# A group norm and a displaced 3x3 filter in one core: the orders of five engines by kind of unit

## The reference

```
g = v.reshape(B_, G, C_ // G, H_, W_)
m = jnp.mean(g, axis=(2, 3, 4), keepdims=True)
s = jnp.var(g, axis=(2, 3, 4), keepdims=True)
v = ((g - m) / jnp.sqrt(s + 1e-5)).reshape(v.shape)
...
shifted = x[:, ch[:, None, None], iyc[:, :, None], ixc[:, None, :]] * mask
kern = jnp.exp(-(kx * kx + ky * ky) / (2.0 * SIGMA * SIGMA))
kern = kern / kern.sum(axis=(1, 2), keepdims=True)
out = lax.conv_general_dilated(shifted, kern_c[:, None], (1, 1), 'SAME', feature_group_count=C)
...
x = x + out
```

## Time and profile before

| | us |
|---|---|
| median of 3 runs | 1114.45 |
| the profiled execution, its own time | 1114.61 |
| its span, first to last instruction | 1112.8 |
| TensorE products, busy | 833.4 |
| VectorE, busy | 835.0 |
| ScalarE, busy | 661.0 |
| GpSimd, busy | 170.7 |
| mean granted TensorE clock | 0.872 of full |

### The profile page before, as it was taken

One profiled execution on the slowest core, in us unless ns is written; L12 is line 12 of the kernel. 1 busy time (PEld: TensorE's weight loads), 2 busy tenths in 40 slices (PEclk: granted clock), 3 DMA queues, 4 the chain that ended last, 5 costly groups with the idle time before them and its releaser, 6 DMA issues. The chain is left out here.

```text
span 1112.8 us, 9630 instructions
## 1 busy us (share of the span) xinstructions
PE 833.4 (75%) x2176; PEld 399.4 (36%) x2176; DVE 835.0 (75%) x565; ACT 661.0 (59%) x547; POOL 170.7 (15%) x204
## 2 busy tenths in 40 slices
PE   6976986678688698759848887888888686888710
PEld 2432433234343244324324443343444343443310
DVE  8187696976948768696784968787887858659685
ACT  0564546565477574766556666556566474666771
POOL 3103131012110303201211110111112101102010
PEclk9988898989799898888969899898999889788955
DMA  9737979898899797989799999999999897997936
GB/s 373 309 148 274 430 291 400 345 382 373 343 403 412 287 429 320 410 328 398 319 347 429 396 402 428 398 429 398 430 398 433 336 426 305 399 431 306 373 160 292
DMA packets 27818, 403.07 MB, mean 362 GB/s; under 512 B 3216, under 2 KB 3216, under 8 KB 3216
## 3 DMA queue, kind: packets, MB, share of 16 engines
q1 hardware_dynamic: 27792, 402.71, 88.6%
HBM read 201.38 MB, written 201.33 MB: 362 GB/s over the span
## 5 line engine op out<-in xcount | busy, mean ns | idle before, releaser
L243 PE MATMUL sum_ps<-xs,bands 128*128 128x512 f32 x1024 | 505.4, 651 | 23.9 <-DMA xs<-x_dram 23.9
L346 ACT ACTIVATE unused<-xs,small 128x4096 bf16 (+1 forms) x96 | 356.1, 3709 | 20.7 <-ACT small L339 7.7
L499 DVE SCALAR_TENSOR_TENSOR smooth<-frame,xs 128x1700 f32 (+5 forms) x96 | 163.6, 1704 | 220.7 <-ACT frame L320 141.6
L243 PEld LDWEIGHTS sum_ps<-xs,bands 128*128 128x128 f32 x1024 | 209.1, 210 | 270.9 <-issue 267.5
L243 PE MATMUL sum_ps<-xs,halves 128*128 128x512 f32 x512 | 246.3, 637 | 74.2 <-DMA xs<-x_dram 74.2
L313 ACT ACTIVATE frame<-xs,small (+1 forms) x96 | 223.4, 2327 | 130.7 <-DVE smooth L502 128.2
L209 POOL TENSOR_TENSOR small<-small 128x3 f32<-128x3 f32 x32 | 60.9, 1902 | 900.3 <-ACT small L352 900.3
L506 DVE SCALAR_TENSOR_TENSOR xs<-smooth,small,xs 128x1700 f32 (+5 forms) x96 | 163.6, 1704 | 36.5 <-POOL small L221 34.0
L243 PEld LDWEIGHTS sum_ps<-xs,halves 128*128 128x128 f32 x512 | 102.3, 204 | 216.8 <-issue 122.8
L502 DVE SCALAR_TENSOR_TENSOR smooth<-frame,xs,smooth 128x1700 f32<-128x1700 f32 (+5 forms) x96 | 163.5, 1704 | 3.4
L509 DVE SCALAR_TENSOR_TENSOR xs<-smooth,small,xs 128x594 f32 (+9 forms) x96 | 159.8, 1665 | 3.4
(11 more groups left out here) (81 smaller groups left out, 279.0 us busy)
## 6 DMA issues: line engine op xcount, KB each, us to landing
xs<-x_dram SPq DMA_DIRECT2D x96, 2048.0 KB, 14.7
out_dram<-xs SPq DMA_DIRECT2D x96, 2048.0 KB, 11.8
smooth<-offset_dram SPq DMA_DIRECT2D x1, 48.0 KB, 4.0
```

The costliest lines, as they stand in the source:

```text
L243: last = nc.tensor.matmul(sum_ps[:, :], (FIRST, SAME, SECOND)[i], slot_px(n, c * BANK, (c + 1) * BANK), start=(i == 0 and c == 0), stop=(i ...
L346: nc.scalar.activation(unused[:, :], xs[:, bass.ds(n % SLOTS * PIX, PIX)], ACT.Square, bias=neg_mean[:, i:i + 1], accum_out=squares[:, i:i ...
L499: V.scalar_tensor_tensor(sm, frame_window(-1), side_w[:, bass.ds(n, 1), 0], frame_window(0), ALU.mult, ALU.add).wait_op(frame_ready, done_ ...
```

## The change

Five edits in one:

1. VectorE loads the word of the next tile (`windows` has one more entry for it) between L499 and L502 of the present one, not ahead of the tile; the addresses of the weights come from one register.
2. ScalarE has two orders. `large_unit` (even units) takes `variances` first, then the fills of tiles 0 and 1 one behind the other, and only then `sum_means` of the next unit. `small_unit` (odd ones) keeps the old order except that the second square goes ahead of the fill of tile 2. The loop runs over pairs. `variances` also waits until the weights of the unit before are all written.
3. SyncE starts the loads in another order: none after the first and third tile of six, two after the second and the sixth, one after the fourth and fifth.
4. TensorE sums one tile of the light unit ahead of the heavy unit's variances and two behind them; around a light unit's variances it stays at two and one.
5. GpSimd makes the weights tile by tile: one operation for the unit and three for each tile, ten in all, and releases each tile by itself.

```diff
@@ SyncE @@
+            AGAIN = [(), (0, 1), (), (2,), (3,), (4, 5)]
             for n in range(TILES):
                 store(n)
-                if 1 <= n <= TILES - SLOTS:
-                    load(n - 1 + SLOTS)
+                for i in AGAIN[n % len(AGAIN)]:
+                    m = n - n % len(AGAIN) + i + SLOTS
+                    if m < TILES:
+                        load(m)
@@ GpSimd @@
                 V.tensor_tensor(rstd0, var, power, ALU.pow).then_inc(rstd_step, 1)
                 pool.wait_ge(rstd_step, STEPS * u + 1)
-                V.tensor_tensor(fix, rstd0, rstd0, ALU.mult).then_inc(rstd_step, 1)
-                ...
-                V.tensor_tensor(col_w[:, now * UT:(now + 1) * UT, :], base_w[:, u * UT:(u + 1) * UT, :],
-                                rstd.unsqueeze(2).to_broadcast([P, UT, 3]), ALU.mult).then_inc(col_w_ready, UT)
+                for i in range(UT):
+                    column = slice(i, i + 1)
+                    V.tensor_scalar(fix[:, column], var[:, column], rstd0[:, column], rstd0[:, column],
+                                    ALU.mult, ALU.mult).then_inc(rstd_step, 1)
+                    pool.wait_ge(rstd_step, STEPS * u + 2 * i + 2)
+                    V.tensor_scalar(rstd[:, column], fix[:, column], -0.5, 1.5,
+                                    ALU.mult, ALU.add).then_inc(rstd_step, 1)
+                    pool.wait_ge(rstd_step, STEPS * u + 2 * i + 3)
+                    if u >= 2 and i == 0:
+                        pool.wait_ge(tile_done, UT * (u - 1) + 1)
+                    V.tensor_scalar(col_w[:, now * UT + i, :], base_w[:, u * UT + i, :], rstd0[:, column],
+                                    rstd[:, column], ALU.mult, ALU.mult).then_inc(col_w_ready, 1)
@@ TensorE @@
             for u in range(UNITS):
+                ahead = 1 if u % 2 == 0 else 2
                 if u + 1 < UNITS:
-                    sums(u + 1, range(UT - 1))
+                    sums(u + 1, range(ahead))
                 variances(u)
                 if u + 1 < UNITS:
-                    sums(u + 1, range(UT - 1, UT))
+                    sums(u + 1, range(ahead, UT))
                     means(u + 1)
@@ ScalarE @@
-            def variances(u):
+            def variances(u, first=False):
                 act.wait_ge(var_ps_ready, u + 1)
+                if not first:
+                    act.wait_ge(col_w_ready, UT * u)
+            def large_unit(u, first=False):
+                variances(u, first)
+                fill_frame(u, 0)
+                next_fill(u, 0)
+                fill_frame(u, 1)
+                next_fill(u, 1)
+                sum_means(u + 1)
+                means(u + 1)
+                square(u + 1, 0)
+                fill_frame(u, 2)
+                next_fill(u, 2)
+                means_to_fill(u + 1)
+                square(u + 1, 1)
+                square(u + 1, 2)
+            def small_unit(u, ahead=True):
                 ...
                 if ahead:
                     means(u + 1)
                     square(u + 1, 0)
+                    square(u + 1, 1)
                 fill_frame(u, 2)
                 if ahead:
                     next_fill(u, 2)
                     means_to_fill(u + 1)
-                    square(u + 1, 1)
                     square(u + 1, 2)
+            with act.Fori(0, UNITS // 2 - 1) as pair:
+                small_unit(act.snap(2 * pair + 1))
+                large_unit(act.snap(2 * pair + 2))
+            small_unit(UNITS - 1, ahead=False)
@@ VectorE @@
                                        ).wait_op(frame_ready, done_count, "sem-ge").then_inc(half_smooth, 1)
+                dve.reg_load(entry, windows[0:1, bass.ds(done, 1)])
                 V.scalar_tensor_tensor(sm, frame_window(1), side_w[:, bass.ds(n, 1), 1], sm,
...
             def tile_of(n):
-                dve.reg_load(entry, windows[0:1, bass.ds(n, 1)])
                 dve.reg_mov(done_count, n + 1)
                 done = dve.snap(done_count, min_val=1, max_val=TILES)
-                weights = dve.snap(n % (2 * UT), min_val=0, max_val=2 * UT - 1)
+                dve.reg_mov(column, n % (2 * UT) * 3)
+                weights = dve.snap(column, min_val=0, max_val=(2 * UT - 1) * 3)
```

More of the change, by code:

```diff
@@ L91, in build @@
         rstd0, fix, rstd = (small[:, 18 + i * UT:18 + (i + 1) * UT] for i in range(3))
-        col_w = small[:, 27:45].rearrange("p (u k) -> p u k", k=3)
+        col_flat = small[:, 27:45]
+        col_w = col_flat.rearrange("p (u k) -> p u k", k=3)
         side_w = xs[:, SLOTS * PIX:SLOTS * PIX + 2 * TILES].rearrange("p (n k) -> p n k", k=2)
         base_w = sb("base_w", [P, TILES, 3])
-        windows = sb("windows", [P, TILES], i32)
+        windows = sb("windows", [P, TILES + 1], i32)
         fills = sb("fills", [P, TILES], i32)
@@ L203, in _ @@
             pool.wait_ge(table_ready, 1)
-            STEPS = 5
+            STEPS = 1 + 2 * UT
             def weights(u):
@@ L380, in _ @@
                 square(0, i, first=(i == 0))
-            unit_of(0)
+            large_unit(0, first=True)
             act.addr_align(256, max_nops=0)
-            with act.Fori(1, UNITS - 1) as u:
-                unit_of(u)
-            unit_of(UNITS - 1, ahead=False)
+            with act.Fori(0, UNITS // 2 - 1) as pair:
+                small_unit(act.snap(2 * pair + 1))
+                large_unit(act.snap(2 * pair + 2))
+            small_unit(UNITS - 1, ahead=False)
         @block.vector
@@ L458, in _ @@
                                     ALU.logical_shift_left))
-            chained(V.tensor_tensor(windows[:, :], parts[:, KIND], parts[:, TO], ALU.bitwise_or))
-            chained(V.tensor_tensor(windows[:, :], windows[:, :], parts[:, FROM], ALU.bitwise_or))
+            chained(V.tensor_tensor(windows[:, 0:TILES], parts[:, KIND], parts[:, TO], ALU.bitwise_or))
+            V.tensor_copy(windows[:, TILES:], parts[:, FROM, 0:1])
+            chained(V.tensor_tensor(windows[:, 0:TILES], windows[:, 0:TILES], parts[:, FROM], ALU.bitwise_or))
             dve.wait_ge(exps_ready, 1)
@@ L483, in _ @@
             done_count = dve.alloc_register("done_count")
+            column = dve.alloc_register("column")
             def smooth_tile(rows, cols, src, dst, n, done, weights):
@@ L505, in smooth_tile @@
                 dve.wait_ge(col_w_ready, done)
-                V.scalar_tensor_tensor(x_window(0, rows), sm, col_w[:, bass.ds(weights, 1), 1], x_window(0, rows),
+                V.scalar_tensor_tensor(x_window(0, rows), sm, col_flat[:, bass.ds(weights + 1, 1)], x_window(0, rows),
                                        ALU.mult, ALU.add
                                        ).wait_op(smooth_ready, done_count, "sem-ge").then_inc(centre_added, 1)
-                V.scalar_tensor_tensor(x_window(1, rows), sm[:, 0:rows - 1], col_w[:, bass.ds(weights, 1), 0],
+                V.scalar_tensor_tensor(x_window(1, rows), sm[:, 0:rows - 1], col_flat[:, bass.ds(weights, 1)],
                                        x_window(1, rows), ALU.mult, ALU.add
                                        ).wait_op(centre_added, done_count, "sem-ge").then_inc(above_added, 1)
-                V.scalar_tensor_tensor(x_window(0, rows - 1), sm[:, 1:rows], col_w[:, bass.ds(weights, 1), 2],
+                V.scalar_tensor_tensor(x_window(0, rows - 1), sm[:, 1:rows], col_flat[:, bass.ds(weights + 2, 1)],
                                        x_window(0, rows - 1), ALU.mult, ALU.add
@@ L540, in _ @@
             dve.reg_mov(slot, 0)
+            dve.reg_load(entry, windows[0:1, 0:1])
             dve.addr_align(256, max_nops=0)
```

1 line of the change is left out of this document (removed).

## The result

The changed kernel takes 1123.19 us, the median of four runs (1121.30 to 1123.59), against 1113.89 for the kernel before on the same chip (four runs, 1113.13 to 1116.01): a ratio of 1.0077, 95% interval 1.0058 to 1.0096, so 0.8% slower. The forecast was 1120.5 us, on a base of 1114.6: a change of +6.0 us, where the medians show +9.3 and the two profiled executions +6.7. The profiled execution took 1121.3 us, the lowest of the four, its span is 1119.1 against 1112.8, and the mean granted clock fell from 0.872 to 0.846.

What follows compares the result with a forecast made beforehand. Bound: a cycle of VectorE's release, ScalarE's squares, TensorE's variance products and last sums, and ScalarE's fills, without loads. Terms 2.2 + 1.9 + 3.9 - 2.0 = +6.0 us on 1114.6 gave 1120.5 us, range 1103 to 1133.

Steps and rivals of the forecast that it cites:

- Where the time is set: Cycle: VectorE's release in the heavy unit, ScalarE's squares, TensorE's variance products and last sums, ScalarE's fills and squares; no load.
- the six periods that the forecast named: Periods of units 4, 6, 12, 14, 24, 26, where ScalarE's sum (L330) comes after VectorE's release.
- Variances ahead of the heavy frame: ScalarE waits 1.8 us more before every heavy frame, VectorE's 1.52 us wait at L506 goes: +2.2 us for 12 heavy units.
- Heavy order: ScalarE fills tile 1 straight behind tile 0; light sum at +12.8, tile 2 later in some heavy units: +1.9 us.
- much slower: Rival: ScalarE's loop of two units and GpSimd's ten operations leave 0.5 us more issue a fill: 1132 us, chance 0.10.
- Pairs outside the four lighter ones, with the last light unit: The forecast's terms outside the four lighter pairs: variances +2.2, heavy order +1.9, last light unit -2.0 us.
- Last light unit: Two VectorE issue gaps shrink by 0.7 us each and a 0.7 us wait for weights goes: -2.0 us.
- The four lighter pairs: From 604 to 847 us: saving unusable, 7.2 us on top, less 3.0 of waits and 0.3 of the sum's place: +3.9 us.
- Loads two at a time: SyncE's loads go some 14 us earlier, but TensorE takes such tiles 8 us or more after landing: 0.
- Weights and word: GpSimd's tile-by-tile weights cost nothing under the heavy frame; VectorE's early word saves 0.7 us a gap, mostly off the cycle.
- The clock's rival: TensorE's shorter waits keep its clock high, sums at 7.1 us: -24 us, about 1097, or half, 1109; chance 0.20.
- Nothing moves: Rival: transfers hold the lighter pairs at 418 GB/s, gains and losses cancel against slack: 1114 to 1116 us, chance 0.18.

Runs made afterwards that it cites:

- e6: The changed kernel with SyncE's order of loads as before: 1115.53 us, ratio 1.0019 to the kernel before.
- e3: The changed kernel with TensorE summing two tiles ahead of every unit's variances, as before the change: 1110.94 us, ratio 0.9986 to the kernel before.
- e11: The changed kernel with SyncE's and TensorE's orders both as before: 1129.87 us, ratio 1.0135 to the kernel before.
- e12: e11 with the heavy unit's variances behind the fill of tile 0: 1094.05 us, ratio 0.9808 to the kernel before.
- e1: The changed kernel with the heavy unit's variances behind the fill of tile 0 again: 1117.32 us, ratio 1.0033 to the kernel before.
- e2: The changed kernel with all three tiles of the next heavy unit summed ahead of the light unit's variance products: 1093.07 us, ratio 0.9818 to the kernel before.
- e4: The kernel before with only the one edit of e2, three tiles summed ahead around light units: 1115.68 us, ratio 1.0022 to the kernel before.
- e5: The changed kernel with TensorE two tiles ahead at heavy units and three at light ones: 1094.55 us, ratio 0.9831 to the kernel before.
- e8: The changed kernel with the table word loaded ahead of its own tile again: 1125.18 us, ratio 1.0094 to the kernel before.
- e7: The changed kernel with GpSimd's six weight operations of before: 1122.85 us, ratio 1.0084 to the kernel before.

## Why the prediction was right, point by point

The four kernels that differ only in two of the edits say it best (medians in us, all with the variances first; the kernel before stood between 1112.9 and 1115.3 beside them):

| | loads as changed | loads as before |
|---|---|---|
| one ahead | 1123.2, ratio 1.0077 (the change) | 1115.5, 1.0019 (e6) |
| two ahead | 1110.9, 0.9986 (e3) | 1129.9, 1.0135 (e11) |

Each new order cures the variances' place by itself (e3, e6); both together do it twice and pay for both. With the variances behind the frame neither is needed (e12: 1094.1 without both, against 1117.3 in e1 with both). So no single edit is the one that loses. The place of `variances` in `large_unit` costs some 5 us beside the two new orders (e1) and 36 without them (e11, e12); the two orders gain some 7 us where the variances stand first (e11 to the change) and cost some 24 where they stand behind the frame (e12 to e1).

- **Where the time is set.** Right. The cycle over squares, variance products, last sums, fills and squares was confirmed by breaking it (e2, -30 us), in four of the six periods that the forecast named; in those of units 4 and 6 the gain was 1.05 and 0.49 us. That no load is in it held for before and after, but not for the neighbours: e4, e5 and e11 are set by loads.
- **Variances ahead of the heavy frame, +2.2 (and 7.2 more in the lighter pairs).** Right in mechanism: 1.81 us more before unit 14, 1.9 in the mean, and the heavy waits at L506 gone. In size it is right only for the part outside the lighter pairs: set back alone (e1) it gives 3.2 to 5.9 us in all, and in the lighter pairs, for which the sum had 7.2 us of it, nothing; there TensorE's order holds the time (e3 takes 4.0 us off them).
- **Heavy order, +1.9.** L341 came at +11.6 in unit 28, not at +12.8, since the first tile's sums were quicker than I took them, and tile 2 of unit 28 started at +20.8 instead of +21.9, so it did not hold the pair up: the light unit behind it began 1.4 us earlier after the heavy start than before (+35.3 against +36.7). The pairs from units 24 and 28 grew by 2.4 and 1.7 us all the same (I had 0.3 and 1.9). In unit 28's the growth comes later: the sum for unit 30 stood 1.6 us behind VectorE's release, where it had been 0.7 ahead of it. So that figure came out by another road than the forecast's. In unit 24's pair 1.2 us of it is ScalarE's issue, for which the sum had nothing beyond the heavy join. The kernel before and then the changed one, ScalarE ahead of the means (the earlier trace rows has the same 0.25):

```profile
895.87 0.17 ACT L335 ACTIVATE small<-mean_ps 128x3 f32<-128x3 f32 x1 [0.25 <-issue]
```

```profile
897.01 0.17 ACT L346 ACTIVATE small<-mean_ps 128x3 f32<-128x3 f32 x1 [0.85 <-issue]
...
909.50 0.20 ACT L350 ACTIVATE small<-small 128x3 f32<-128x3 f32 x1 [0.87 <-issue]
```

  The second place stood at 0.26 us before. That is the rival "much slower" at a part of its size: 0.6 us in two places of the few pairs where these stand behind a late fill.
- **Pairs outside the four lighter ones, with the last light unit**: 2.2 + 1.9 - 2.0 = +2.1 was the sum; measured from heavy start to heavy start they grew by 2.1 in all and the first start came 0.9 later, +3.0. Inside it the sizes are scattered, from -2.15 (unit 2's pair, the fill no longer behind a late sum) to +2.39 (unit 24's).
- **Last light unit, -2.0.** Wrong: it took 21.88 us before and 21.73 after, -0.15. The wait of 0.7 us for weights stayed (0.69 and 0.67), the two issue gaps shrank by 0.2 each and not by 0.7, and 0.3 us came in between the first two operations of the second tile. In e8, with the word's load put back, the unit takes 22.26. So of the +3.0 above, +3.2 is everything else, for which the sum had +4.1: two misses that cancel.
- **The four lighter pairs, +3.9**: -0.51, +0.49, +0.86 and +2.43, together +3.3. The mechanism is the forecast's in its first half: the heavy unit's sum came at +37.7 to +39.5 (I had +38.3), 1.0 to 3.8 us behind VectorE's release, so the saving could not be used. The 1.8 us ahead of the frame were booked on top of that, and e1 shows that they are not a cost of the frame's place here.
- **Loads two at a time, 0.** Wrong by itself: e6 puts it at some +7 with TensorE's new order, and e11 against e3 at -19 with the old one. By the ratios it is +6.5 and -16.6. Transfers hide or gate by the order that consumes them; I costed this edit against the consumer of the kernel before. The example was misread too: the store of tile 17 took 20.1 us to land and not some 12 (it began at 252.43 and landed at 272.5), so the load of tile 26 came 10 us earlier in the changed kernel (268.1) and not 14.
- **Weights and word, near 0.** Right (e7, e8), but for the last light unit. The Trainium skill (SBUF — State Buffer, Who interferes with whom), by which GpSimd stands behind VectorE's two-input instructions, fits the new operations' times: 0.81, 0.62 and 0.63 us in the mean of 96 each. The 158 of these 288 that ran with VectorE idle took 0.19 to 0.34 us (the forecast used 0.20 for all), and the 102 that began well inside such a VectorE instruction all ended 0.05 to 0.22 us behind its end. They had the heavy frame to hide in.
- **The clock's rival.** It did not come: the sums behind the products took 9.38 us in the heavy pair and 8.81 in three of the four lighter ones, only one of the fifteen took 7.11 (two before), and the mean clock fell. The forecast put the 9.72 us of before down to the lower clock as a whole; the trace has a granted clock of 0.50 from 502.44 to 507.00 only and of 0.93 from 507.00 to 512.16.
- **Nothing moves.** Refuted by the interval.

So the total was right within 3 us, and the two groups of pairs within 1 us each. The heavy frame's delay, the late light sum and the unusable saving are what the forecast said. The closeness of the total is in part luck: 1.9 us of gain in the last light unit did not come, the loads were put at nothing and cost some 7, and the 7.2 us booked on the frame in the lighter pairs are no cost of that place. And the sum was right for one combination of edits only; my expectations for e3, e4, e5, e6, e11 and e12, which each took the cure or the load off one place, missed their ranges by 5 to 23 us.

Left open: why the early loads cost 7 us where TensorE does not need them; which of the edits left in e12 (word, weights, ScalarE's orders but for the variances) makes it 21 us faster than the kernel before; and the kernel with two ahead, the new loads and the variances behind the frame, which was not run.

## What to carry to other kernels

Do not put an operation that waits for another engine ahead of one that is ready and on the cycle, in order to save a wait further down: here it traded 1.5 us for 1.9 and hung the frame on whatever the other engine does first (36 us in the worst case). In an engine with a fixed order, look for long work that stands behind a short wait and could run inside it; moving the sums there gave 30 us (e2), and nothing where the loads were not early enough (e4). And cost orders that feed each other as a table of combinations, not as a list: the same new order of loads gained 17 to 19 us or lost 6 to 8, by TensorE's order beside it.

## What the runs showed of the hardware

The same 16 products of 128x512 took 7.0 to 7.1 us in 65 of the 96 tiles of the changed kernel and 8.5 to 10.0 in the others (up to 10.2 in other runs). The changed kernel around unit 14 (columns as in the earlier trace rows): the stretch of the variance products with their waits, the sums behind it (as a whole, then its start and its end), and the sums after those. A transfer counts in the stretch in which it starts, so the DMA share of a short stretch can come out above 1:

```profile
492.50:497.50 5.00, 2.31 (x10) 2.22 (x11) 4.86 (x5) 4.83 (x5) 0.00 (x0) 0.50 1.05 377
497.50:506.80 9.30, 9.30 (x17) 3.82 (x17) 7.27 (x6) 1.68 (x3) 6.53 (x8) 0.75 1.02 403
499.50:501.50 2.00, 2.00 (x4) 0.86 (x3) 1.71 (x2) 0.21 (x1) 1.52 (x2) 0.50 1.05 451
503.50:506.80 3.30, 3.30 (x8) 1.14 (x6) 3.23 (x3) 0.00 (x0) 3.13 (x3) 1.00 1.11 382
508.36:515.50 7.14, 7.11 (x18) 2.93 (x17) 4.24 (x5) 5.74 (x5) 0.18 (x1) 1.00 1.02 438
```

After two waits of 4.49 and 2.53 us the granted clock is 0.50 (1.2 GHz), and it comes back to 1.00 (2.4 GHz) only on the way through 9.3 us of unbroken products: it is still 0.50 up to 501.5, 1.00 from 503.5, and 0.75 in the mean. So here the idle time ahead of a long group costs twice, once for itself and 2.3 us (9.38 against 7.11) for the group. The rule is not simply that any idle time costs: 7.13 us were also seen straight after a wait of 1.03 us for a load (e4, at 629.25), through which the granted clock stayed at 1.00.
